# A four-block graph network on one core: the output constant moves into VectorE's copy, the third hop's norm writes in place

## The reference

```python
edge_index = jnp.stack([src, dst])
h = relu(layernorm(x));  x = x + L0(h)   # three weighted graph convolutions, then a product
h = relu(layernorm(x));  x = x + L1(h)   # below
h = relu(layernorm(x));  x = x + L2(h)   # six rounds of mean over neighbours, product, relu
h = relu(layernorm(x));  x = x + L3(h)   # gcn_conv, tanh, then  h @ W2 + b2
return x

# L1: the mean over incoming edges of (row of the source + features of the edge)
m = h[src] + edge_features
hv_new = segment_sum(m, dst) / maximum(deg, 1.0)
h = (1.0 + eps) * h + hv_new             # then W1, batch norm, relu, W2, batch norm, relu

# L3, of a node that is no edge's destination:  tanh(h @ W1 + b1) @ W2 + b2
```

## Time and profile before

| | |
|---|---|
| Time, median of 3 runs | 3292.27 us (3290.51 to 3295.48) |
| The profiled execution, its own time | 3287.36 us |
| Its span, first to last instruction | 3285.6 us |
| Busy: TensorE, VectorE, ScalarE, GpSimd | 2527.2, 2032.4, 1972.3, 1442.2 us |
| Granted TensorE clock, mean | 0.882 |

### The profile page before, as it was taken

The page is one execution under the profiler, slowest core; times in us unless marked ns, Lnnn a source line. Parts: engine busy times, 40 slices in busy tenths (PEclk is TensorE's granted clock), DMA queues, the critical chain, the costliest instruction groups (busy, mean ns, idle before and its releaser), DMA issues. The chain is left out here.

```text
span 3285.6 us, 46019 instructions
## 1 busy us (share of the span) xinstructions
PE 2527.2 (77%) x11251; PEld 1564.2 (48%) x11251; DVE 2032.4 (62%) x7784; ACT 1972.3 (60%) x4381; POOL 1442.2 (44%) x1507
## 2 busy tenths in 40 slices
PE   5767755558777678899999945799999999876840
PEld 2444434435555456445455422365655656543520
DVE  6544555558889766233333356687887878776630
ACT  1666755557777766455555558877777776764400
POOL 5555454545645264000000000176766767554576
PEclk8888877789888898899999966899999999987875
DMA  4655533445566565333333458866656656433311
GB/s 94 173 158 154 170 109 111 121 119 163 165 179 195 173 193 168 108 137 134 137 134 134 137 183 268 282 186 185 192 177 189 186 175 191 146 116 112 96 57 41
DMA packets 528965, 504.91 MB, mean 154 GB/s; under 512 B 58706, under 2 KB 389955, under 8 KB 528616
## 3 DMA queue, kind: packets, MB, share of 16 engines
q1 hardware_dynamic: 477388, 415.73, 39.2%
q0 software_dynamic: 47184, 85.73, 10.5%
q10 hardware_dynamic: 4172, 0.99, 0.2%
HBM read 246.45 MB, written 260.27 MB: 154 GB/s over the span
## 5 line engine op out<-in xcount | busy, mean ns | idle before, releaser
L1854 POOL DMA_INDIRECT h_G<-step_tab,row_i x294 | 287.1, 977 | 350.1 <-DMA step_tab<-l_NR 192.9
L1854 POOL DMA_INDIRECT h_M<-step_tab,row_i x294 | 284.3, 967 | 119.3 <-issue 86.3
L1567 DVE TENSOR_SCALAR b_Y<-b_BP,col 128x512 f32<-128x512 f32 x148 | 109.9, 742 | 354.5 <-PE b_BP L1521 354.5
L804 PE MATMUL a_PA<-a_H,w 128*128 128x512 f32 x504 | 263.2, 650 | 70.2 <-ACT a_H L968 63.4
L1549 ACT ACTIVATE b_Z<-b_BQ,bn 128x512 f32<-128x512 f32 x148 | 115.0, 777 | 256.7 <-PE b_BQ L1513 256.4
L1521 PE MATMUL b_BP<-b_Z,w 128*128 128x512 f32 x592 | 266.3, 592 | 0.0
L1609 POOL TENSOR_TENSOR b_d<-b_d,neghalf 128x1 f32<-128x1 f32 x1 | 0.6, 565 | 592.4 <-DVE b_d L1600 592.4
L2221 DVE TENSOR_TENSOR_SCAN h_T<-keep,h_T,h_P 128x512 f32<-128x512 bf16 x196 | 222.9, 1137 | 11.3 <-PE h_P L1972 2.1
L270 POOL DMA_INDIRECT h_G<-msg_tab,row_i x147 | 143.8, 978 | 195.5 <-issue 132.1
L239 ACT ACTIVATE a_NR<-a_XR,a_ln_nm,a_ln_rs 128x128 f32<-128x128 f32 x392 | 155.9, 485 | 106.3 <-DVE a_ln_nm L222 106.3
L239 ACT ACTIVATE a_HI<-a_X,a_ln_nm,a_ln_rs 128x128 f32<-128x128 f32 x490 | 201.0, 484 | 23.2 <-DVE a_ln_nm L222 23.2
(11 more groups left out here) (385 smaller groups left out, 6503.9 us busy)
## 6 DMA issues: line engine op xcount, KB each, us to landing
b_HI<-hin_tab SPq DMA_DIRECT2D x148, 256.0 KB, 2.8
y_tab<-b_Y SPq DMA_DIRECT2D x148, 256.0 KB, 2.0
l_Y<-y_tab SPq DMA_DIRECT2D x148, 256.0 KB, 4.0
l_X<-x_tab SPq DMA_DIRECT2D x148, 256.0 KB, 4.6
x_tab<-a_X SPq DMA_DIRECT2D x112, 256.0 KB, 4.3
hin_tab<-a_HI SPq DMA_DIRECT2D x112, 256.0 KB, 3.1
a_XR<-in_x SPq DMA_DIRECT2D x97, 256.0 KB, 4.5
out_rows<-l_O SPq DMA_DIRECT2D x97, 256.0 KB, 3.1
```

The lines of the kernel that those rows point to most:

```text
L804: nc.tensor.matmul(PA[b][:, 0:nt * P], w[:, :], h[b][:, 0:nt, :].rearrange("p t d -> p (t d)"), start=True, stop=True).then_inc(done, 1)
L1567: nc.vector.tensor_scalar(Y[b][:, :], BP[b][:, :], col[:, C_B12:C_B12 + 1], None, ALU.add).then_inc(b_y, 1)
L1854: pool.indirect_dma_start(out=GR_[i % 2][b][:, k, :], out_offset=None, in_=table[:, :], in_offset=bass.IndirectOffsetOnAxis(ap=row_i[:, t ...
```

## The change

1. `rows_const` is gone. The constant b2 is broadcast once into an SBUF tile rb32 by one more load (30 in place of 29) on ScalarE's queue, and VectorE adds it as it copies a pair's bank out: a tensor_tensor with rb32 repeated over the four rows in place of a copy. Each matmul of `rows` now carries the stop flag.
2. `m_apply` writes its rows in place, in RS, after waiting until the store of x from RS has landed; HR and its waits are gone; `m_store` reads RS.
3. `m_scaled` is gone. In hop 3 VectorE multiplies by vscale in the message: 4 or 3 scalar_tensor_tensor on 128 x 128 (`RS * vscale + gathered`) first, then the addition of the features in one tensor_tensor of 128 x 512 or 128 x 384.

```diff
--- before.py
+++ after.py
@@ -141,6 +141,7 @@
...
     rbh = sb(top, "rbh", [P, D])
+    rb32 = sb(top, "rb32", [P, D])
     split_x1 = sb(top, "split_x1", [3, 512], BF16)
@@ -291,11 +292,14 @@
...
             if self.kind == "mean":
+                dve.wait_ge(mn.normed, 2 * i + b + 1)
+                for j in range(nt):
+                    last = nc.vector.scalar_tensor_tensor(rows[:, j, :], RS[:, t + j, :], vscale[:, t + j:t + j + 1], rows[:, j, :],
+                                                          ALU.mult, ALU.add)
+                last.then_inc(h_mid, 1)
+                dve.wait_ge(h_mid, 2 * i + b + 1)
                 dve.wait_ge(features_in[b], 16 * (i + 1))
-                nc.vector.tensor_tensor(rows[:, 0:nt, :], rows[:, 0:nt, :], features[b][:, 0:nt, :], ALU.add).then_inc(h_mid, 1)
-                dve.wait_ge(h_mid, 2 * i + b + 1)
-                dve.wait_ge(m_v, 2 * i + b + 1)
-                last = nc.vector.tensor_tensor(rows[:, 0:nt, :], rows[:, 0:nt, :], RS[:, t:t + nt, :], ALU.add)
+                last = nc.vector.tensor_tensor(rows[:, 0:nt, :], rows[:, 0:nt, :], features[b][:, 0:nt, :], ALU.add)
             last.then_inc(h_msg, 1)
@@ -453,7 +457,7 @@
...
     sp_f, sp_r = (XDW[1][0:1, b, :, :] for b in range(2))
-    HR, MH, FE = SN[0], R1, R2
+    MH, FE = R1, R2
     PA, P3 = [ps(ctx, f"a_PA{b}") for b in range(2)], [ps(ctx, f"a_P3{b}") for b in range(2)]
@@ -488,13 +492,12 @@
...
 
-    xd_got, xd_st, xd_ld, wd_set, m_x1_st, m_h_st, m_v = ([sems(f"xd_got{k}", 2) for k in range(2)], [sems(f"xd_st{k}", 2) for k in range(2)], sems("xd_ld", 4),
-                                                                 sem("wd_set"), sems("m_x1_st", 4), sems("m_h_st", 2),
-                                                                 sem("m_v"))
+    xd_got, xd_st, xd_ld, wd_set, m_x1_st, m_h_st = ([sems(f"xd_got{k}", 2) for k in range(2)], [sems(f"xd_st{k}", 2) for k in range(2)], sems("xd_ld", 4),
+                                                            sem("wd_set"), sems("m_x1_st", 4), sems("m_h_st", 2))
     feat_in, feat_pad, mh_st, mh_ones = sems("feat_in", 2), sem("feat_pad"), sems("mh_st", 2), sem("mh_ones")
...
     REST = E - FULL * P
-    N_LOADS = 29
+    N_LOADS = 30
     padded = [(t, base) for t in (hin_tab, x1_tab) for base in (E0, S0)]
@@ -591,7 +594,8 @@
...
                     sp.wait_ge(mn.normed, 2 * i + b + 1)
-                    sp.dma_start(edge_rows(msg_tab[3], RR, first_tile(i, b), nt), HR[b][:, 0:nt, :]).then_inc(m_h_st[b], 16)
+                    t = first_tile(i, b)
+                    sp.dma_start(edge_rows(msg_tab[3], RR, t, nt), RS[:, t:t + nt, :]).then_inc(m_h_st[b], 16)
 
@@ -917,6 +921,7 @@
...
                      (rbl[:, :], b0l.partition_broadcast(P)), (rbh[:, :], bh.partition_broadcast(P)),
+                     (rb32[:, :], b32.partition_broadcast(P)),
                      (w01[:, :], W01[:, :]), (w02[:, :], W02[:, :]),
@@ -995,18 +1000,8 @@
...
                     t = first_tile(i, b)
-                    after(act, m_v, 2 * (i - 1) + b + 1)
-                    after(act, m_h_st[b], 16 * i)
-                    mn.act_apply(act, i, b, _Rows(RS, t), HR[b])
-
-            def m_scaled(i):
-                for b, nt in enumerate(SUB):
-                    t = first_tile(i, b)
                     act.wait_ge(m_x1_st[2 * (i % 2) + b], 16 * (i // 2 + 1))
-                    act.wait_ge(mn.normed, 2 * i + b + 1)
-                    for k in range(nt):
-                        last = nc.scalar.activation(RS[:, t + k, :], HR[b][:, k, :], AF.Copy, scale=vscale[:, t + k:t + k + 1])
-                    last.then_inc(m_v, 1)
+                    mn.act_apply(act, i, b, _Rows(RS, t), _Rows(RS, t))
 
@@ -1061,8 +1056,6 @@
...
                         sn.act_std(act, i + 1)
-                    if hop.h == 2 and i > 1:
-                        m_scaled(i - 2)
                     if hop.h == 2 and u:
@@ -1071,9 +1064,7 @@
...
                 if k == GAP[3]:
-                    m_scaled(IT - 2)
                     m_apply(IT - 1)
-                    m_scaled(IT - 1)
             ln2.act_std(act, NS - 1)
@@ -1946,17 +1937,13 @@
...
 
-            def rows_const(j):
-                for b in range(2):
-                    nc.tensor.matmul(XB[j % 2][b][:, :], ones3[:, :], split_out[:, :], start=False, stop=False, skip_group_check=True)
-
             def rows(j):
...
                     for k in range(4):
-                        last = nc.tensor.matmul(XB[j % 2][b][:, k * P:(k + 1) * P], HT[b][:, k, :], w32[:, :], start=False, stop=(k == 3), skip_group_check=True)
+                        last = nc.tensor.matmul(XB[j % 2][b][:, k * P:(k + 1) * P], HT[b][:, k, :], w32[:, :], start=False, stop=True, skip_group_check=True)
                     last.then_inc(p2_set, 1)
@@ -2020,8 +2007,6 @@
...
                     prod(late)
-                if late is not None:
-                    rows_const(late)
                 for i in its[:1]:
@@ -2191,7 +2176,8 @@
...
                     dve.wait_ge(o_st[b], o_stores(j, b))
-                    nc.vector.tensor_copy(O[b][:, :, :].rearrange("p t d -> p (t d)"), XB[r][b][:, :]).then_inc(o_set, 1)
+                    nc.vector.tensor_tensor(O[b][:, :, :], XB[r][b][:, :].rearrange("p (t d) -> p t d", d=D),
+                                            rb32[:, :].unsqueeze(1).broadcast_to([P, 4, D]), ALU.add).then_inc(o_set, 1)
 
```

## The result

The changed kernel takes 3284.03 us (median of 16 runs, 3277.66 to 3288.91), the kernel before 3291.32 (16 runs beside them). The ratio is 0.9974, interval 0.9966 to 0.9981: 8.6 us faster, 6.3 to 11.2. Forecast: -8.7 us and 3283.5. Two profiled executions have spans of 3282.4 and 3273.4 us, two of before 3285.6 and 3295.4. That scatter is wider than what is looked for, so the stages are compared, over all profiles at hand. The windows and timelines shown first are those of the first profile, whose span is 3282.4 us.

What follows compares the result with a forecast made beforehand. Bounds: VectorE in hop 2, ScalarE in the gap, a loop in hop 3, GpSimd in the waves. Terms -4.1 - 1.0 + 0 - 1.5 - 2.1 = -8.7 us, forecast 3283.5 us, range 3274 to 3293.

Steps and rivals of the forecast that it cites:

- The gap, -4.1: First gap slot: two of ScalarE's scalings ahead of a_H leave the path, 2 x 2.04 = 4.1 us faster.
- bound of another 2.8 us: Gap: at most 2.8 us more if TensorE's eight products after the idleness ran at 2.4 GHz; mostly thought unlikely.
- Rival B: Gap: the gain is given back behind another DMA, -4.6 us remain, 3287.7; chance 0.24 together with another rival.
- Hop 3, -1.0: Hop 3's messages: four instructions hide in each of six feature waits, -2.5 us, first slot and end +0.75 each.
- rival C: Hop 3: VectorE decides, its added work counts in full, +10.5 there, +2.8 us in all, 3295.1; chance 0.08.
- -0.72 for the norm of the dense step: Hop 3, behind the features: one addition instead of two, 1.33 us becomes 0.61, so a_ln_nm comes 0.72 us earlier.
- +0.31 for the second half: Hop 3, a message's second half: three scalar_tensor_tensor in place of one addition with RS cost 0.31 us more.
- The 20 us more on GpSimd: Hop 3: new instructions with two SBUF inputs stretch gathers by 0.29 us each, at most 20 us, covered by GpSimd's free time.
- Waves 0 to 4, 0: Waves 0 to 4: TensorE loses the constant's products but only waits longer for gathers, so 0 us gained.
- rival A: Waves: TensorE bounds them, so all removed products show, -26.0 - 5.1 us, 3261; chance 0.07.
- rival D: Waves: the new additions hold up some ten gathers a wave by 0.29 us, +17 less 8.7, 3301; chance 0.04.
- Waves 5 and 6, -3.6: Waves 5 and 6: removed products shorten TensorE's path, -1.5 us in wave 5 and -2.1 in wave 6.

Runs made afterwards that it cites:

- features_first: The changed kernel, but hop 3's messages wait for and add the features first, as before, then the scalar_tensor_tensor; 3290.45 us, ratio 0.9996 against the kernel before.
- Unscaled: The changed kernel without vscale in hop 3's messages: 28 additions of RS in place of 98 scalar_tensor_tensor; 3283.99 us, ratio 0.9979 against the kernel before.
- const_end: The changed kernel with the constant's two products put back for nine pairs of waves 5 and 6, on top of VectorE's addition; 3286.54 us, ratio 0.9986 against before.

## Why the prediction was right, point by point

The time and the sum were right; of the terms one was right in place and size, one right in its reason and too large, two off in opposite directions. So the sum's closeness is in part luck. And the stated range, 3274 to 3293, holds "no change" too, so that the time lies in it says little; the measured 6.3 to 11.2 around the forecast's 8.7 says more.

- **The gap, -4.1.** Right: 30.8 to 26.2 in nearly every profile, -4.6, and the two idle times 4.1 shorter. Of the half microsecond beyond, TensorE's eight products give 0.15 (5.40 us after 5.55); the stretch's clock is 0.91 after 0.86. The forecast's bound of another 2.8 us, for products that would now run at 2.4 GHz, was met in part in one execution: features_first has 3.89 us for them and 24.5 for the gap. The scalings taken out of hop 2 were worth nothing, as said (that stage took 163.1 to 164.2 us in five profiles with them, 162.2 to 164.4 in nine without). Rival B is out.
- **Hop 3, -1.0.** The reasons held: the wait for the features swallowed the four instructions, the order is worth 5 to 7 us (features_first), and VectorE's added 9.8 us didn't show (rival C is out). The size didn't come: 136.2 us on average in the five profiles with the old messages, 136.8 in the seven with the new ones in this order that scale. The steps "-0.72 for the norm of the dense step" and "+0.31 for the second half" were both counted in full. Unscaled (136.4, no gain where -3.4 was forecast) speaks for it that what VectorE does behind the first half of a message isn't in the loop; with stage lengths that spread over 134.9 to 138.4 in one and the same order, a microsecond isn't shown either way. The 20 us more on GpSimd that were weighed as the most for the new instructions didn't come: hop 3's 98 gathers took 94.4 us in all, 96.7 before. Of them 19 met a scalar_tensor_tensor of the messages and no addition of two SBUF tiles, and they took 0.94 to 0.99 us, where the 49 that met none of these took 0.94; the rows' 0.29 us isn't seen behind these short instructions.
- **Waves 0 to 4, 0.** Right that TensorE doesn't bound them (rival A is out) and that the new addition holds up no gather (rival D): of 11 gathers of the changed kernel that met L2179 alone, the longest took 0.96 us. That agrees with the rule of the Trainium skill's page "SBUF — State Buffer" (section "Who interferes with whom") weighed in the prediction. The addition's own price, and one such pair:

```profile
2383.44 1.28 DVE L2179 TENSOR_TENSOR l_O<-l_XB,rb 128x512 f32<-128x512 f32 x2
...
2398.32 0.95 POOL L1845 DMA_INDIRECT h_G<-step_tab,row_i  x1 [0.30 <-issue]
2398.45 0.69 DVE L2179 TENSOR_TENSOR l_O<-l_XB,rb 128x512 f32<-128x512 f32 x1 [2.81 <-PE l_XB L1946]
```

  What I hadn't thought of: less work on TensorE is also more waiting on TensorE, and at times a lower clock behind it. These waves take 3.4 us more on average, with a spread of 8, and the pauses of after are 13.0 to 15.1 us, not 13 each.
- **Waves 5 and 6, -3.6.** The place was right and the size too small: -6.7 by the means, of which wave 5 gives 1.2 (1.5 forecast), wave 6 4.8 (2.1 forecast), and the stretch behind the last long wait 0.6 (0 forecast). const_end gives +3.0 to +4.0 for the products themselves, which is near the forecast. What the other 2.7 us in wave 6 come from is open; with the same code this part of wave 6 spreads over 3.4 us in one group and 4.3 in the other, so a part of them may be chance.
- **The whole.** The forecast for the norm's part was -5.1, measured -7.2 (-10.2 to -4.6); for the constant's -3.6, measured -1.3 (-4.9 to +2.0). In the stages the norm's part shows 4.6 us in the gap and none in hop 3; what goes beyond stands in the end (471.4 and 471.6 us against before's 473.8 and 477.3), whose code it doesn't touch. The sum hit because both errors fit in the runs' scatter and have opposite signs. That the constant's part gains anything isn't shown by times: its interval holds 0.

## What to carry to other kernels

Ask of each wait what can be put ahead of it: the same 98 instructions cost nothing that shows in front of a DMA's landing and 5 to 7 us behind it. Work taken from an engine that has just enough to do isn't simply free or gained: here taking it away gave about a microsecond (-4.9 to +2.0) and adding as much cost seven (3.0 to 11.2). When an edit in one stage succeeds and the total doesn't move, look at the stages behind it before dropping it, and take more than one profile: a single one would have seemed to prove a loss of 5 us in waves 0 to 4 that the next did not have.

## What the runs showed of the hardware

- After TensorE had stood for 2.00 us in a stretch that was otherwise busy, its granted clock was 0.57 over the next 4 us, and 128 x 512 products took 2.82 us for four instead of 1.98. But a stand of 2.47 us in another execution left the clock at 1.00 and the products at 1.99, and in seven profiles of the waves the clock stayed at 1.00 behind 30 of 42 stands of 1.3 to 2.6 us. The stand alone doesn't decide.
- A stretch at 1.2 GHz can be long: 12 us of wave 5 at a clock of 0.50 with TensorE busy for 11.73 of them. It came at the same place in both profiles of the kernel before, though these began the wave at 2811.9 and 2818.0 us.
- A VectorE addition of a PSUM bank and a repeated SBUF row took what the copy took (two 1.28 us), and left a gather beside it at 0.95 us; of 11 gathers that met it alone the longest took 0.96.
